# Packed spectral transforms, doubled keys and DMA-turned values in a gated cross-attention kernel

## The reference

```python
qf = fft(layernorm(x)); kf = fft(ctx)              # over the 64 positions
corr = ifft(qf * conj(kf)).real
w, idx = top_k(corr, 8); w = softmax(w)
for i in range(8):
    out += w[i] * ctx[min(idx[i] + pos, 63)]       # last row repeated past the end
x = x + tanh(g_xattn) * out
gate, up = layernorm(x) @ W_gate.T, layernorm(x) @ W_up.T   # 512 -> 1792
x = x + tanh(g_ffn) * ((silu(gate) * up) @ W_down.T)
```

## Time and profile before

| | |
|---|---|
| median of three runs | 225.96 us |
| profiled execution: its own time | 226.68 us |
| its span, first to last instruction | 224.8 us |
| mean granted TensorE clock | 0.991 |
| TensorE matmul busy | 215.2 us, 96% |
| VectorE, GpSimd, ScalarE busy | 138.3, 137.7, 111.0 us |

### The profile page before, as it was taken

How to read it: one execution, slowest core, us unless ns; L and a number is a source line. 1 busy time by engine, 2 the same in 40 slices (tenths; PEclk the granted TensorE clock), 3 DMA queues, 4 the chain that set the end, 5 groups by cost and what they waited for, 6 DMA issues and landing times.

```text
span 224.8 us, 6753 instructions
## 1 busy us (share of the span) xinstructions
PE 215.2 (96%) x2779; PEld 148.4 (66%) x2779; DVE 138.3 (61%) x407; ACT 111.0 (49%) x208; POOL 137.7 (61%) x165
## 2 busy tenths in 40 slices
...
GB/s 152 335 434 425 388 140 50 4 3 47 47 4 51 0 50 0 50 3 23 28 25 26 23 73 3 23 143 70 4 26 93 26 0 3 25 73 50 0 3 47
DMA packets 19918, 16.69 MB, mean 74 GB/s; under 512 B 15920, under 2 KB 16304, under 8 KB 19504
## 3 DMA queue, kind: packets, MB, share of 16 engines
...
...
## 4 chain that ended last, share of the span: by engine, by line
PE 86%; DVE 6%; DMA 2%; issue 2%; POOL 1%; ACT 1%; SPq 0%; DVEq 0%; ACTq 0%
PE psum L802 44%; PE psum L967 20%; PE psum L785 10%; PE psum L918 4%; PE psum L903 2%; DMA ctx_sb<-ctx 2%; DVE probs L696 1%; DVE raw_stats L640 1%; PE psum L793 1%; PE psum L885 1%; PE psum L866 1%; ACT xn L537 1%; DVE x_sb L745 1%; PE psum L867 1%; PE psum L868 1%
## 5 line engine op out<-in xcount | busy, mean ns | idle before, releaser
L802 PE MATMUL psum<-xt_hi,wg 128*128 128x128 f16 (+1 forms) x504 | 54.0, 213 | 0.0
L802 PE MATMUL psum<-xt_hi,wu 128*128 128x128 f16 (+1 forms) x504 | 53.9, 213 | 0.0
L802 PE MATMUL psum<-xt_lo,wg 128*128 128x128 f16 (+1 forms) x504 | 53.9, 213 | 0.0
L802 PE MATMUL psum<-xt_lo,wu 128*128 128x128 f16 (+1 forms) x504 | 53.8, 213 | 0.0
L527 POOL TENSOR_TENSOR hid_lo<-hid,hid_hi 128x512 f16<-128x512 f32 (+2 forms) x32 | 33.0, 1037 | 29.0 <-ACT hid_hi L631 29.0
L802 PEld LDWEIGHTS psum<-xt_hi,wg 128*128 128x128 f16 x504 | 44.8, 98 | 6.2 <-issue 5.5
L802 PEld LDWEIGHTS psum<-xt_hi,wu 128*128 128x128 f16 x504 | 44.9, 98 | 3.0 <-issue 2.1
L802 PEld LDWEIGHTS psum<-xt_lo,wu 128*128 128x128 f16 x504 | 45.0, 98 | 0.8
L802 PEld LDWEIGHTS psum<-xt_lo,wg 128*128 128x128 f16 x504 | 45.1, 98 | 0.7
L967 PE MATMUL psum<-wd,hid_hi 128*128 128x512 f16 x112 | 42.5, 379 | 0.1
L967 PE MATMUL psum<-wd,hid_lo 128*128 128x512 f16 x112 | 42.4, 379 | 0.0
...
## 6 DMA issues: line engine op xcount, KB each, us to landing
...
```

The lines of the kernel that those rows point to most:

```text
L802: last = nc.tensor.matmul(psum[:, bank, a * n:(a + 1) * n], w[:, k, m * P:(m + 1) * P], xt[:, e, k, tok], start=(k == 0 and part == 0), st ...
```

## The change

The two halves of the frequencies (even ones, of the 64-point transform, and odd ones, half a step further) are packed in one matrix of 128 columns. One `kspec` with the matrix `values` = [even, odd_v] gives both the key spectrum (rows 0 to 63) and the value spectrum; one `wspec` with `weights` = [even, odd] gives both spectra of the weights. `vspec` and the second `wspec` are gone from pair 1 on. The query matrix is [even, even_turned]. Since the key product still needs 128 rows, ScalarE writes the 64 key rows of both batches twice, to partitions 0 to 63 and 64 to 127 (`kcopy`, two 64x1024 copies), and the packed spectrum once (`vcopy`, one 128x1024 copy). The turned value rows are made by a new step `turn` on SyncE's queue: four DMAs from SBUF to SBUF that swap groups of 32 partitions (31, 32, 32 and 32 rows of 4 KB), and one that reads the last context row from HBM. The loads of pairs 4 to 7 move behind `turn` of pair 1. `sub` and `sum` are cut in two steps each (`sub`, `sub8`; `total`, `mask`), and `exp` in `exp` and `exp8`. `mixed` has one buffer where it had two. The whole `ORDER` is another one, and `WARM_UP` changes. Pair 0 keeps its f32 transforms.

```diff
-FORWARD = ("even_kv", "even", "odd_v", "odd")
+FORWARD = ("query", "values", "weights")
...
-warm:0 stats1:0 rstd1:0 kspec:0 q_norm:0 qspec:0 kcopy:0 kcopy:0.1 vspec:0 prod:0 stats1:1 k_hi:1 lags:0
+warm:0 stats1:0 rstd1:0 kspec:0 q_norm:0 vspec:0 kcopy:0 kcopy:0.1 qspec:0 stats1:1 vcopy:0 k_hi:1 rstd1:1
...
+exp:0 match:0 q_lo:1 lags:0.1 warm:0.1 exp8:0 kcopy:1 mask:0 total:0 vcopy:1 max:0.1 scale:0 kcopy:1.1
+stats1:2 wt:0 match:0.1 rstd1:2 w_hi:0 qspec:1 sub8:0.1 wspec:0 sub:0.1 prod:1 q_norm:2 wspec:0.1 mix_prod:0
...
+qspec:5 out:1 w_rows_hi:4 mix:3 prod:5 k_hi:6 mix:3.1 w_t:4 w_rows_lo:4 prod:5.1 mix:3.2 p_hi:5 gate:2.1
+residual:3 p_hi:5.1 turn:4 p_lo:5 h_hi:2 p_lo:5.1 up:2.1 tanh:2.1 w_t:4.1 silu:2.1 rstd2:3 lags:5 hid:2.1
...
+tanh:4 h_lo:3.3 w_rows_hi:6 up:4 silu:4 m_lo:5.2 m_hi:5.3 w_t:6 prod:7 prod:7.1 p_hi:7 m_lo:5.3 down:3.2
+turn:6 p_hi:7.1 p_lo:7 down:3.3 w_rows_lo:6 mix:5 out:3 mix:5.1 p_lo:7.1 w_t:6.1 mix:5.2 hid:4 gate:4.1
+residual:5 lags:7 rstd2:5 tanh:4.1 up:4.1 silu:4.1 xn:5 max:7 x_rows_hi:5 wspec:6 sub8:7 h_hi:4 x_t:5
...
+h_lo:4.2 down:4.1 tanh:5 m_hi:6.3 silu:5 scale:7 up:5 m_lo:6.2 w_rows_hi:7 w_t:7 h_lo:4.3 down:4.2 hid:5
+m_lo:6.3 turn:7 down:4.3 w_rows_lo:7 mix:6 out:4 w_t:7.1 mix:6.1 mix:6.2 gate:5.1 residual:6 store:4 up:5.1
+rstd2:6 tanh:5.1 silu:5.1 xn:6 wspec:7 hid:5.1 h_hi:5 gate:5.2 x_rows_hi:6 h_lo:5 x_t:6 x_rows_lo:6 up:5.2
...
-WARM_UP = ((12, 4), (3, 7), (2, 7))
+WARM_UP = ((12, 4), (6, 7), (0, 7))
...
-    kv_spec = sb("kv_spec", [P, 2, 4, D])
+    v_spec = sb("v_spec", [P, 2, 2, D])
+    v_turned = sb("v_turned", [P, 2, 2, D])
+    k_spec = sb("k_spec", [P, 2, 2, D])
...
-            load(ctx_sb, cv, 4, PAIRS, ctx_loaded[4])
-            load(x_sb, xv, 4, PAIRS, x_loaded[4])
             for step, p, n in order:
                 e = p % 2
+                if step == "turn":
+                    sp.wait_ge(v_copied, copies(p))
+                    if p > 2:
+                        sp.wait_ge(mixed_done, 4 * p - 4)
+                    for to, first, count in ((1, 33, 31), (32, 0, 32), (64, 96, 32), (96, 64, 32)):
+                        sp.dma_start(v_turned[to:to + count, e, :, :], v_spec[first:first + count, e, :, :])\
+                          .then_inc(v_moved[e], 16)
+                    sp.dma_start(v_turned[0:1, e, :, :], last_rows[p:p + 1, :, :]).then_inc(v_moved[e], 16)
+                    if p == 1:
+                        load(ctx_sb, cv, 4, PAIRS, ctx_loaded[4])
+                        load(x_sb, xv, 4, PAIRS, x_loaded[4])
...
+                if step == "vcopy" and p > 0:
+                    act.wait_ge(k_spectra, p + 1)
...
+                    nc.scalar.activation(v_spec[:, e, :, :], psum[:, k_bank(p, 0):k_bank(p, 1) + 1, :], ACT.Copy,
+                                         scale=SPEC).then_inc(v_copied, 1)
+                if step == "kcopy" and p > 0:
+                    act.wait_ge(k_spectra, p + 1)
...
+                    nc.scalar.activation(k_spec[rows(n), e, :, :], psum[0:L, k_bank(p, 0):k_bank(p, 1) + 1, :], ACT.Copy,
                                          scale=SPEC).then_inc(k_copied, 1)
...
+                if step == "mix_prod" and p > 0:
+                    m, b = n // 2, n % 2
+                    dve.wait_ge(w_spectra, nth("wspec", p))
+                    if m == 0:
+                        dve.wait_ge(v_copied, copies(p))
+                    else:
+                        dve.wait_ge(v_moved[e], nth_turned(p))
+                    if p == 1:
+                        dve.wait_ge(mix_done, last_of("residual", 0))
+                    else:
+                        dve.wait_ge(*split_count("m_lo", p - 1, n))
+                    nc.vector.scalar_tensor_tensor(mixed[:, n, :], psum[:, w_bank(p, m, b), :], MIX_UP,
+                                                   (v_spec, v_turned)[m][:, e, b, :], ALU.mult, ALU.mult)\
+                      .then_inc(mixed_done, 1)
...
                 if step == "wspec" and p > 0:
...
+                    transform([w_bank(p, 0, b) for b in range(2)], "weights", w_hi[:, e, :], w_lo[:, e, :])\
                         .then_inc(w_spectra, 1)
```

More of the change, by code:

```diff
@@ L118 @@
[L118 to L142, removed]
@@ L143 @@
-exp:5 m_lo:4.1 wspec:4.1 q_hi:6 kspec:6 mix_prod:4.2 down:2.3 mix_prod:4.3 m_hi:4.2 sum:5 kcopy:6 gate:3
-m_lo:4.2 kcopy:6.1 out:2 m_hi:4.3 scale:5 up:3 tanh:3 m_lo:4.3 w_rows_hi:5 silu:3 w_t:5 gate:3.1 w_rows_lo:5
-q_lo:6 mix:4 tanh:3.1 mix:4.1 w_t:5.1 silu:3.1 mix:4.2 vspec:6 residual:4 up:3.1 vcopy:6 vcopy:6.1 hid:3
-rstd2:4 qspec:6 wspec:5 prod:6 gate:3.2 mix_prod:5 p_hi:6 prod:6.1 xn:4 p_lo:6 mix_prod:5.1 p_hi:6.1 up:3.2
-hid:3.1 tanh:3.2 p_lo:6.1 x_rows_hi:4 silu:3.2 h_hi:3 x_t:4 wspec:5.1 h_hi:3.1 h_lo:3 gate:3.3 mix_prod:5.2
@@ L148 @@
-x_rows_lo:4 lags:6 hid:3.2 tanh:3.3 m_hi:5 up:3.3 silu:3.3 h_lo:3.1 x_t:4.1 m_hi:5.1 down:3 store:0 h_hi:3.2
-m_lo:5 hid:3.3 m_hi:5.2 mix_prod:5.3 down:3.1 max:6 h_lo:3.2 m_hi:5.3 h_hi:3.3 sub:6 h_lo:3.3 gate:4 k_lo:7
-match:6 m_lo:5.1 down:3.2 tanh:4 exp:6 m_lo:5.2 up:4 sum:6 m_lo:5.3 stats1:7 scale:6 down:3.3 silu:4 kspec:7
-rstd1:7 out:3 mix:5 hid:4 kcopy:7 mix:5.1 kcopy:7.1 mix:5.2 w_rows_hi:6 vspec:7 residual:5 h_hi:4 w_t:6
-gate:4.1 q_norm:7 rstd2:5 up:4.1 tanh:4.1 w_rows_lo:6 vcopy:7 silu:4.1 xn:5 gate:4.2 w_t:6.1 vcopy:7.1 hid:4.1
@@ new lines @@
+p_lo:1.1 scale:0.1 wt:0.1 residual:0 lags:1 w_hi:0.1 wspec:0.2 max:1 rstd2:0 wspec:0.3 sub:1 k_lo:2 xn:0
+match:1 xt:0 q_lo:2 x_hi:0 k_hi:3 mix_prod:0.1 kspec:2 exp:1 k_lo:3 mix_prod:0.3 mix:0.2 mask:1 kcopy:2
+mix:0.3 sub8:1 x_lo:0 turn:1 exp8:1 kcopy:2.1 total:1 gate:0 residual:0.1 scale:1 vcopy:2 stats1:3 w_rows_hi:1
+rstd2:0.1 qspec:2 tanh:0 w_t:1 up:0 prod:2 w_rows_lo:1 prod:2.1 p_hi:2 silu:0 p_hi:2.1 p_lo:2 gate:0.1 hid:0
+xn:0.1 w_t:1.1 stats1:4 p_lo:2.1 h_hi:0 xt:0.1 x_hi:0.1 turn:2 rstd1:3 lags:2 tanh:0.1 x_lo:0.1 silu:0.1
@@ new lines @@
+p_hi:3.1 stats1:5 p_lo:3 xn:1 wspec:2 hid:0.3 x_rows_hi:1 p_lo:3.1 down:0.1 h_hi:0.3 x_t:1 mix_prod:2 k_hi:4
+mix_prod:2.1 x_rows_lo:1 m_hi:2 mix_prod:2.2 lags:3 m_hi:2.1 h_lo:0.3 m_hi:2.2 mix:2 max:3 x_t:1.1 m_lo:2
+down:0.2 sub8:3 sub:3 exp8:3 m_lo:2.1 k_hi:5 down:0.3 match:3 q_hi:4 k_lo:4 exp:3 gate:1 total:3 m_lo:2.2
+mask:3 mix_prod:2.3 up:1 scale:3 tanh:1 m_hi:2.3 silu:1 w_rows_hi:3 m_lo:2.3 out:0 kspec:4 w_t:3 hid:1 mix:2.1
+w_rows_lo:3 vcopy:4 stats1:6 mix:2.2 gate:1.1 residual:2 kcopy:4 rstd1:5 kcopy:4.1 w_t:3.1 q_lo:4 up:1.1
```

239 lines of the change are left out of this document (140 added, 99 removed).

## The result

The changed kernel takes 230.35 to 230.98 us in the three runs that are compared, against a median of 226.04 (225.72 to 226.48) for the kernel before: a ratio of 1.020, with a 95% interval of 1.018 to 1.023. It is slower by 4.6 us, where 218.9 was predicted. Two more of its five runs took 235.1 us, one of them the profiled one (span 233.0), and are left out of the comparison as slow, as are single runs of e1 and e10 and four of e5; the profiles of e1 (219.6 us) and e5 (229.6 us) are such runs too.

What follows compares the result with a forecast made beforehand. TensorE's work was taken to bound the kernel from 58.6 us on, latency before that; -7.3 - 2.3 + 1.0 + 0.5 + 1.0 = -7.1 us gave 218.9 on the median, range 215.5 to 221.0 (chance 0.60), high end 223.5 with rivals.

Steps and rivals of the forecast that it cites:

- Turning by DMA: SyncE's queue, pairs 4 to 7: transposes behind the turn cost nothing to 1.8 us at pair 6, 0.5 in all.
- The port rule of the Trainium skill: Turning DMAs on 32 partitions reach only 8 of 16 DMA ports; sum 1 to 2 us worse at pairs 6, 7.
- Rival (b): SyncE's queue costs 1.5 to 2 us at pairs 4 to 7, +3 on the forecast: 221.9; chance 0.07.
- The range's high end: Whole kernel: 223.5 us, set to take in three rivals of 222.9, 221.9 and 221.4 us.
- The prediction's own sign of being wrong: TensorE idle above 3 us after 60 us, or the head ending more than 3 us later.
- (d): Slower: the relay through ScalarE, GpSimd and VectorE becomes a pair's period, 26.5 us; kernel 228 to 233; chance 0.11.
- Transforms taken away: TensorE, 14 groups of 6 matmuls gone: -7.3 us in the saturated stretch, -2.3 before 58.6 us.
- The head and the first pairs: Before gate:1: head +1.0 us from later queries and wide copies, -2.3 from three transform groups gone.
- what the prediction left open: Head, 26 to 30 us: whether the slow-clock stretch comes again, 1.6 us either way; kept as it was.
- Copies: ScalarE, later pairs: wide copies of 1.06 us add 1.1 us a pair, 7.4 over the kernel, hidden.
- The order, and the port: Later pairs: TensorE waits from short hand-offs and VectorE's long two-input lines, 1.0 us, ends 0 and 8.4.
- (a): GpSimd's queue and VectorE's port add 0.6 us of TensorE idle to each of 7 pairs: +4, 222.9; chance 0.15.

Runs made afterwards that it cites:

- e1: The changed kernel without the turn's five DMAs, products reading the unturned values, and ScalarE's wait for them gone: 216.5 us, 0.957 of the kernel before.
- e10: The changed kernel with the turn as four unturned DMAs over all 128 partitions, a quarter of the columns each, no last row: 219.2 us, 0.975.
- e5: The changed kernel with the turn's four DMAs (31 and 3 x 32 rows) each taking every fourth partition, values not turned: 226.2 us, 0.999.
- e7: The changed kernel with cosine and sine rows interleaved, turning by two DMAs (63 and 64 rows) and the last row, result unchanged: 217.4 us, 0.963.
- e12: The changed kernel with the turn's DMAs issued from ScalarE's queue, the transposes staying on SyncE's: 244.5 us, 1.082 of the kernel before.
- e4: The changed kernel with the turn as one DMA of all 128 partitions (512 KB), values not turned: 218.0 us, 0.964 of the kernel before.
- e9: e7 with the two 1 MB loads of pairs 4 to 7 issued before all steps: 217.9 us, 0.964 of the kernel before.
- e11: The changed kernel with the turn as two unturned DMAs of partitions 1 to 63 and 64 to 127, and the last row: 218.0 us, 0.965.
- e6: The changed kernel with the turn's four blocks of partitions (31 and 3 x 32 rows) copied straight, not exchanged: 231.6 us, 1.026.
- e2: The changed kernel with the five late turn steps moved in the order, behind transposes they had stood ahead of: 221.4 us, 0.978.

## Why the prediction was wrong, step by step

**Turning by DMA: the step that failed.** It put 0.5 us; the change takes about 14 us more than e1 (230.7 by the median of its compared runs, and 216.5 by e1's). The prediction had looked at the right queue and the right pairs, with a sound form: cover of 6.6 us at pair 6 against a need of 5.3 to 8.4. (The high end counts the 1.2 us of the issue twice, since landings are counted from the issue; by its own rows it is 7.2.) The size of the need was wrong. It took the transpose's landing, 2.4 to 4.3 us, from a kernel in which no such copy was moved beside it, and asked only whether the values land in time. But the turn is a load on engines that the transposes need too. From the turn's first issue to the transpose's landing the need was 153.6 - 142.8 = 10.8 us at pair 6, and 106.4 - 95.25 = 11.1 at pair 4. Of that, the turn's rows hold the engines for some 7 us, 3 of them with one row moving at a time. Three idles of 8.7 us follow, and the lower clock after two of them, which the prediction did not price: 2.74 for 1.40 us of 12 transforms, 1.47 for 0.75 of 6, and 6.40 us for 96 matmuls of gate and up that take 5.47 in e7, 3.0 us in all. And turn:3 stood ahead of x_t:1, a place that the prediction didn't list; gate:1 came 4.1 us later than in e7. Over both parts: 4.1 + (164.2 - 152.3) = 16.0 us between the profiles of the change and e7, measured from gate:1 to the last matmul (65.50 to 229.71 and 61.41 to 213.67). The port rule of the Trainium skill, quoted ahead of the result for 1 to 2 us, pointed at the right DMAs and the right sign, but not the size: it treats the four alike, and the records show single rows in file.

Rival (b), the queue of SyncE, is the one that happened in kind, with a size four times over what it was given (221.9, chance 0.07) and a second place before gate:1; and e12 shows that being in one queue is not what makes the transposes late. The range's high end, 223.5, was built from landings of the kernel before, and so could not hold it. The prediction's own sign of being wrong, more than 3 us of idle on TensorE after 60 us, came true with 10.3. That the kernel is slower was forecast by (d) at 0.11, but not by this mechanism.

**Transforms taken away: right.** From gate:1 to the last matmul 159.02 us before and 152.25 in e1, 152.3 in e7: 6.8 us less, where 7.3 less the 1.0 for waits in the order was put.

**The head and the first pairs: right as a sum in these two profiles.** +1.0 - 2.3 would start gate:1 at 61.3; e7 starts it at 61.41, e1 at 61.97. prod:0 came at 9.53 (9.5 put), wspec:0 at 17.02 (17.2). With the turn's term taken out, the prediction's sum is 218.4 on the median, where e1 has 216.5 and e7, which does turn, 217.4. The rest lies at least in part in what the prediction left open, the lower clock in the head. From 20 to 35 us the granted clock was 0.77 in the profile of e1 and 0.89 in that of e7. In those of e4, e9 and e11 it was 1.00, and gate:1 started at 59.39, 58.69 and 59.66.

**Copies: right.** A wide copy takes 1.01 us (1.06 put), ScalarE's total grew by 6.6 us (7.4 put), hidden, in two groups (busy, mean ns of one | idle before):

```profile
L646 ACT ACTIVATE k_spec<-psum 64x1024 f32<-64x1024 f32 x14 | 14.2, 1013 | 8.0 <-PE psum L870 7.8
L638 ACT ACTIVATE v_spec<-psum 128x1024 f32<-128x1024 f32 x7 | 7.1, 1010 | 0.9 <-PE psum L870 0.9
```

Half the partitions are not half the price.

**The order, and the port: 0.6 us of idle where 1.0 was put, and no rival.** The contention is there (groups of the change):

```profile
L778 DVE SCALAR_TENSOR_TENSOR probs<-probs,expo 128x512 f32<-128x512 f32 x7 | 7.6, 1087 | 0.0
L755 DVE TENSOR_TENSOR expo<-top 128x64 f32<-128x64 f32 x7 | 3.4, 479 | 0.1
```

The two together are 7 x (1.087 + 0.479) = 11.0 us, where they were 7 x (0.911 + 0.616) = 10.7: one got slower, the other faster. In e1 and e7 it is 10.7 and 10.6, and TensorE idles 0.6 us in e1's stretch from 58.6. Rivals (a) and (d) both fall: that the order was laid out without regard to the port cost next to nothing here. No run took the port's contention itself away, so that is read from e1 and e7, not from an experiment on it.

**Open.** That the DMA of 31 rows is the dear one is read from the packets and not tested; four DMAs of 32 rows, with the last row put in afterwards, would do it. Why e5 beats e6 by 5 us with the same numbers of rows is measured, not explained. Nor is a second stall. TensorE stops in the middle of one run of matmuls, with all its operands there, while turn:2 is moved (last bracket: idle before):

```profile
39.37 0.19 PE L887 MATMUL psum<-xt_hi,wu 128*128 128x64 f16 x1
40.97 0.19 PE L887 MATMUL psum<-xt_lo,wu 128*128 128x64 f16 x1 [1.41 <-issue]
```

It is there in e6 (39.20, 2.21 us), e2 (38.81, 1.73) and, shorter, e11 (0.51), and in none of e1, e5 and e7. A supply of instructions that shares the DMA engines would fit; this is argued only.
